# Moving the first mask to ScalarE's DMA queue and redrawing the orders of four engines in a gated cross-attention kernel

## The reference, cut to what matters

```
x        [4, 256, 256]     ctx [4, 1601, 256]     mask [4, 1601] (bytes, one row per batch)
w_gating [2, 256, 1024]    w_linear [1024, 256]   g_xattn, g_ffn: one number each

h      = layernorm(x)
scores = h @ ctx^T / 16, and -1e30 where mask is 0
out    = softmax(scores) @ ctx            (zero if a batch has no key at all)
x      = x + tanh(g_xattn) * out
h2     = layernorm(x)                     (then rounded to fp8 e4m3, as are weights and activations)
x      = x + tanh(g_ffn) * ((gelu(h2 @ w_gating[0]) * (h2 @ w_gating[1])) @ w_linear)
```

## Time and profile before

| | |
|---|---|
| median of 3 runs | 132.19 us (131.89 to 133.86) |
| the profiled execution's own time | 132.56 us |
| its span, first to last instruction | 130.7 us |
| busy: PE / PEld / DVE / ACT / POOL | 123.8 / 106.9 / 102.5 / 77.2 / 87.8 us |
| chain that ended last | PE 81%, DVE 8%, ACT 3%, DMA 3% of the span |
| granted TensorE clock | 1.0 in all 40 slices |
| read from HBM | 11.57 MB |

### The profile page before, as it was taken

The page is one execution under the profiler, slowest core; times in us unless marked ns, Lnnn a source line. Parts: engine busy times, 40 slices in busy tenths (PEclk is TensorE's granted clock), DMA queues, the critical chain, the costliest instruction groups (busy, mean ns, idle before and its releaser), DMA issues.

```text
span 130.7 us, 2554 instructions
## 1 busy us (share of the span) xinstructions
PE 123.8 (95%) x887; PEld 106.9 (82%) x887; DVE 102.5 (78%) x242; ACT 77.2 (59%) x142; POOL 87.8 (67%) x136
## 2 busy tenths in 40 slices
PE   6866999999999999999999999999999999999991
PEld 4545899899999996899999899999989894345780
DVE  3643899687999799995799498999786998966662
ACT  3266478688586799563465896943884306755300
POOL 3077989769939999789999605999949705920000
PEclk9999999999999999999999999999999999999999
DMA  3989998800400316900005000001400000000233
GB/s 103 274 225 367 393 358 347 258 19 3 160 5 0 100 63 212 353 5 0 0 5 160 0 0 0 8 0 7 154 0 5 0 0 0 0 5 10 70 121 120
DMA packets 6915, 12.77 MB, mean 98 GB/s; under 512 B 884, under 2 KB 4728, under 8 KB 6904
## 3 DMA queue, kind: packets, MB, share of 16 engines
q1 hardware_dynamic: 6904, 12.62, 29.0%
HBM read 11.57 MB, written 1.05 MB: 97 GB/s over the span
## 4 chain that ended last, share of the span: by engine, by line
PE 81%; DVE 8%; ACT 3%; DMA 3%; issue 1%; SPq 1%; ACTq 0%; DVEq 0%
PE ring L646 15%; PE pv L678 9%; PE pv L686 9%; PE pv L682 9%; PE scores L660 9%; PE scores L663 8%; PE scores L664 8%; PE scores L707 7%; PE ring L723 5%; DMA cn<-in_ctx_dram 3%; DVE cT_lo L509 2%; ACT cT_hi L422 1%; DVE negm L496 1%; DVE xn L548 1%; ACT gate L449 1%
## 5 line engine op out<-in xcount | busy, mean ns | idle before, releaser
L379 POOL TENSOR_TENSOR chl<-cn,chl 128x256 fp32r<-128x256 f32 (+1 forms) x52 | 37.5, 759 | 7.0 <-ACT chl L429 7.0
L509 DVE TENSOR_TENSOR cT_lo<-ring,cT_hi 128x512 fp32r<-128x512 f32 (+1 forms) x28 | 16.7, 627 | 6.7 <-ACT cT_hi L422 6.7
L663 PE MATMUL scores<-cT_lo,xT_hi 128*128 128x512 f32 (+2 forms) x64 | 21.7, 347 | 0.0
L509 DVE TENSOR_TENSOR pT_lo<-ring,pT_hi 128x512 fp32r<-128x512 f32 (+1 forms) x32 | 18.0, 582 | 4.7 <-ACT pT_hi L422 4.7
L422 ACT ACTIVATE pT_hi<-ring 128x512 fp32r<-128x512 f32 (+1 forms) x32 | 15.5, 511 | 10.5 <-PE ring L646 10.3
L664 PE MATMUL scores<-cT_hi,xT_lo 128*128 128x512 f32 (+2 forms) x64 | 21.7, 345 | 0.0
L422 ACT ACTIVATE cT_hi<-ring 128x512 fp32r<-128x512 f32 (+1 forms) x28 | 14.7, 548 | 9.8 <-PE ring L646 9.8
L660 PE MATMUL scores<-cT_hi,xT_hi 128*128 128x512 f32 (+2 forms) x64 | 18.7, 374 | 1.1 <-ACT cT_hi L422 1.1
L678 PE MATMUL pv<-chl,pT_hi 128*128 128x256 f32 (+1 forms) x104 | 19.2, 297 | 0.0
L387 POOL TENSOR_TENSOR ws<-ws,wc 128x256 f32<-128x256 f32 x24 | 16.2, 707 | 3.8 <-DVE wc L558 3.8
L435 ACT ACTIVATE sp<-sp,nb,sr 128x1024 f32<-128x1024 f32 (+1 forms) x16 | 16.8, 1053 | 1.3 <-DVE nb L525 1.3
(11 more groups left out here) (68 smaller groups left out, 198.4 us busy)
## 6 DMA issues: line engine op xcount, KB each, us to landing
cn<-in_ctx_dram SPq DMA_DIRECT2D x11, 512.0 KB, 7.8
ws<-in_L_ffn_w_gating_dram SPq DMA_DIRECT2D x4, 512.0 KB, 6.8
ws<-in_L_ffn_w_linear_dram SPq DMA_DIRECT2D x2, 512.0 KB, 3.9
out_dram<-xs SPq DMA_DIRECT2D x8, 128.0 KB, 1.7
mrow<-in_mask_BxS_bk_dram SPq DMA_DIRECT2D x4, 200.1 KB, 6.5
xs<-in_x_dram SPq DMA_DIRECT2D x1, 768.0 KB, 9.7
cn<-in_ctx_dram SPq DMA_DIRECT2D x2, 256.0 KB, 3.4
cn<-in_ctx_dram SPq DMA_DIRECT2D x4, 65.0 KB
```

The lines of the kernel that those rows point to most:

```text
L379: last = nc.gpsimd.tensor_tensor(chl[b % 2][0:parts, t, D:2 * D], cn[b % 2][0:parts, t, :], chl[b % 2][0:parts, t, 0:D].bitcast(f32), ALU. ...
L509: nc.vector.tensor_tensor(dst, bank_view(f, size), hi.bitcast(f32), ALU.subtract).then_inc(lo_ready, 1)
L663: nc.tensor.matmul(dst, xT_hi[:, j % (2 * QT), k, :], cT_lo[:, k, cols], start=False, stop=False)
```

## The change

The first mask is no longer loaded by SP between ctx groups 1 and 2. ACT issues it as its first instruction, ahead of everything else on its queue. The second mask moves on SP from behind batch 1's context to behind the first weight piece. All four orders are drawn anew. Cut to its core (each order changes throughout; two lines stand for them):

```diff
     PE_ORDER = """
-        X0:0 X0:1 C0:1 C0:0 S0:0 C0:2 C0:3 C0:4 S1:0 C0:5 S0:1 C0:6 S1:1 X1 S0:2 S0:3 C1:1 C1:0 S1:2 S1:3
+        X0:0 C0:0 X0:1 C0:1 C0:3 C0:2 S1:0 C0:5 C0:6 S1:1 S0:0 C0:4 S0:1 C1:3 C1:0 X1 S0:2 S0:3 S1:2 C1:1
...
     POOL_ORDER = """
-        Z0:0 B0 Z0:1 Z0:3 F1 F0 Z0:2 B1 I0 Z1:1 Z1:3 I1 Z1:2 Z1:0 Z2:3 B2 F2 F3 Z2:1 B3 Q0 I2 Z2:0 Z2:2 Q1
-        Z3:0 I3 Z3:1 Z3:2 Z3:3 Q2 I4 Q3 I5"""
+        F0 B0 Z0:1 Z0:2 Z0:3 Z0:0 F1 B1 I0 Z1:3 I1 Z1:0 Z1:2 Z1:1 F2 B2 Z2:1 Z2:3 Z2:0 Q0 F3 B3 I2 Z2:2 Q1
+        I3 Z3:0 Z3:1 Z3:2 Z3:3 Q2 I4 Q3 I5"""
...
             load_ctx(0, 0)
             load_ctx(0, 1)
-            load_mask(0)
             load_ctx(0, 2)
             load_ctx(0, 3)
             sp_eng.dma_start(xs[:, QT:J, :], x_v[:, QT:J, :]).then_inc(x_in, 16)
             for g in range(NG):
                 load_ctx(1, g)
-            load_mask(1)
...
             load_w(0)
+            load_mask(1)
             load_w(1)
...
+            actor.dma_start(mrow[:, 0, :], mask_BxS2_bk0[0:1, :].broadcast_to([P, K])).then_inc(m_in[0], 16)
             gated = False
             for s in act_order:
```

More of the change, by code:

```diff
@@ L60, in gated_cross_attention_ffn @@
-        S6:3 V4:1 P5:2 P5:1 S7:0 V4:2 S7:2 V4:3 S7:1 P6:1 P6:0 V5:0 S7:3 N1 P6:3 V5:1 V5:2 V5:3 P6:2 P7:3 H0
-        V6:0 P7:1 V6:1 P7:0 V6:2 V6:3 H1 P7:2 V7:0 V7:1 V7:2 V7:3 H2 H3 N2 H4 H5 H6 N3 H7 H8 H9 H10 H11 H12
-        Y0 H13 H14 Y1 H15 Y2 Y3 Y4 Y5 Y6 Y7"""
-    ACT_ORDER = """
[L66 to L71, removed]
@@ L74, in gated_cross_attention_ffn @@
-    DVE_ORDER = """
[L75 to L80, removed]
+        X0:0 C0:0 X0:1 C0:1 C0:3 C0:2 S1:0 C0:5 C0:6 S1:1 S0:0 C0:4 S0:1 C1:3 C1:0 X1 S0:2 S0:3 S1:2 C1:1
@@ new lines, in gated_cross_attention_ffn @@
+        C1:2 S1:3 C1:5 S2:0 P0:0 S2:1 C1:4 P0:1 S3:0 V0:0 C1:6 P0:2 S3:1 P0:3 P1:1 V0:1 P1:0 C2:2 S2:2 C2:1
+        S2:3 P1:2 V0:2 P1:3 C2:0 S3:2 V0:3 S3:3 X2 C2:6 V1:0 C2:5 C2:4 C2:3 V1:1 P2:2 V1:2 V1:3 P2:3 S5:0
+        P2:1 P3:0 S4:0 P2:0 P3:1 X3 S4:1 S5:1 C3:1 V2:0 P3:3 V2:1 S5:2 C3:3 V2:2 V2:3 P3:2 S5:3 S4:2 C3:0
+        S4:3 V3:0 C3:2 C3:6 C3:4 V3:1 V3:2 C3:5 P4:3 V3:3 S6:0 P4:0 N0 P4:1 S6:1 S6:2 P4:2 S6:3 V4:0 P5:3
+        V4:1 S7:0 P5:0 V4:2 N1 V4:3 P6:1 S7:2 P5:2 P6:0 S7:1 P5:1 P6:2 V5:0 S7:3 V5:1 V5:2 V5:3 H0 P7:0 P7:1
@@ new lines, in gated_cross_attention_ffn @@
+        V6:0 P7:2 V6:1 P6:3 V6:2 P7:3 V6:3 H1 H2 V7:0 V7:1 V7:2 V7:3 H3 H4 H5 N2 H6 N3 H7 H8 H9 H10 H11 H12
+        H13 Y0 Y1 H14 H15 Y2 Y3 Y4 Y5 Y6 Y7"""
+    ACT_ORDER = """
+        X0:0 C0:0 X0:1 C0:1 R0:1 C0:3 C0:2 R0:3 C0:6 C0:5 R0:2 K1 C0:4 R0:0 C1:3 C1:0 X1 R1:2 C1:1 C1:2 E0:0
+        C1:5 E1:1 E1:0 P0:0 C1:4 E0:1 P0:1 C1:6 P0:2 R1:1 P0:3 P1:1 R1:3 K2 P1:0 C2:2 C2:1 P1:2 R1:0 P1:3
+        C2:0 E2:1 X2 C2:6 C2:5 E2:0 C2:4 C2:3 P2:2 E3:0 K3 R2:3 P2:3 P2:1 P3:0 R2:1 P2:0 R2:2 P3:1 X3 E3:1
+        R2:0 C3:1 P3:3 C3:3 P3:2 C3:0 E5:1 C3:2 E4:1 C3:6 E4:0 C3:4 C3:5 P4:3 P4:0 N0 R3:1 P4:1 R3:3 R3:2
+        P4:2 P5:3 E5:0 E6:1 E6:0 P5:0 N1 P6:1 R3:0 P5:2 P5:1 P6:0 P6:2 E7:0 E7:1 H0 P7:0 P7:1 P6:3 P7:2 P7:3
+        H1 H2 H3 H4 N2 H5 H6 N3 H7 H8 H9 H10 H11 H12 H13 H14 H15"""
@@ new lines, in gated_cross_attention_ffn @@
+    DVE_ORDER = """
+        G0:0 G0:1 X0:0 C0:0 X0:1 C0:1 C0:3 C0:2 C0:6 G1 C0:5 M1:0 C0:4 M0:0 C1:3 C1:0 X1 M0:1 C1:1 C1:2 M1:1
+        C1:5 W0 W1 P0:0 C1:4 G2 P0:1 C1:6 P0:2 M2:0 P0:3 P1:1 M3:0 P1:0 C2:2 C2:1 M2:1 P1:2 A0 P1:3 C2:0 X2
+        C2:6 M3:1 C2:5 G3 C2:4 U0 C2:3 P2:2 A1 P2:3 P2:1 P3:0 U1 W2 P2:0 P3:1 M5:0 X3 P3:3 C3:1 M4:0 A2 M5:1
+        P3:2 C3:3 C3:0 M4:1 U2 C3:2 C3:6 L0 C3:4 C3:5 P4:3 A3 U3 P4:0 M6:0 P4:1 M6:1 P4:2 L1 W3 P5:3 P5:0 A4
+        P6:1 P5:2 P5:1 M7:0 M7:1 W4 P6:0 A5 P6:2 U4 H0 P7:0 P7:1 U5 P6:3 A6 W5 L2 P7:3 P7:2 H1 U6 H2 A7 U7
+        H3 H4 L3 H5 H6 H7 H8 H9 H10 H11 Y0 H12 Y1 H13 H14 Y2 H15 Y3 Y4 Y5 Y6 Y7"""
```

## The result

| | before | after |
|---|---|---|
| median | 132.12 us (131.89 to 133.86) | 133.65 us (132.79 to 134.09, four executions) |
| profiled execution, its span | 132.56, 130.7 us | 133.42, 131.6 us |

The ratio is 1.013, with an interval of 1.010 to 1.016: slower by 1.3%, where 0.5% was forecast. The experiments came in three groups (runs 1 to 4, 5 to 8 and 9 to 12), each with its own executions of before (medians 131.55, 131.99 and 132.13); compare within a group. Executions that took over 1.5% longer than the fastest of the same kernel (one of 136.17 us of the control among them) are left out of the ratios.

The account below looks back on a forecast made before the run. PE, busy 123.8 of 130.7 us, was taken as the bound, its continuous run opened by group 2's landing. 132.56 + 0.2 + 0 + 0.4 = 133.2, or 132.8 on the median's footing; 8 in 10 range 131.2 to 134.5.

Parts of the forecast that it names:

- the forecast case: Whole kernel: the summed terms hold, 132.8 us on the median's footing, from 132.1 to 133.6; chance 0.5.
- its own signs: Profile after: prediction wrong if group 2 lands a microsecond off or a batch change shows an unnamed PE wait.
- On ACT it is free: Start: the mask's 0.43 us issue, moved from SP to ACT, costs nothing, ACT being idle 2.88 us before its first copy.
- I take 0.6, since nothing else in that early stretch is as slow: Start: the mask in front pushes back x and group 0 by 0.6 us, or 1.7 at the old slump's rate; covered.
- I keep its landing at 11.9: Start: context group 2 lands at 11.9 us as before, the bytes ahead of it being the same.
- Rival 1: Start: the slump goes with the mask, landings, PE's run and G1 come 1.3 us earlier, 131.5 us; chance 0.22.
- Start: +0.2: Start: PE's run begins at 12.1 as before, then X1 waits 0.2 us for DVE near 18.5.
- Middle: 0: Batch changes: the old hole at G3 goes (-0.3), a new wait of 0.3 us opens at P0:3 near 32.
- I see it covered: Middle: the old 0.3 us hole behind G3 vanishes, two weighted sums now standing beside G3.
- End: +0.4: End: N3 at T + 4.7 (T: V7's end), H4's bank free only after A7; PE waits 1.0, regains 0.6.
- Rival 2: DVE comes late to fills: G2's place costs 1.3 not 0.3, the end's 0.6 isn't regained, 134.4 us; chance 0.18.
- Rival 3: Start: the mask in front holds up x and group 0, at most 1.7 us against 1.9 cover; 133.3; chance 0.05.

Follow-up runs that it names:

- the control: The changed kernel itself, measured again unaltered: 134.00 us, ratio 1.018 to the kernel before.
- run 4: The changed kernel without any load of the first mask, VectorE setting its bytes to 1: 134.05 us, ratio 1.018 to the kernel before.
- runs 10 and 11: The changed kernel with an unread 200 KB load in the first mask's place: 128 different rows (135.94 us), then one row 128 times (133.72 us).
- run 6: The changed kernel with 22 instead of 15 warm-up matmuls on zeros: 132.89 us, ratio 1.012 to the kernel before.
- Run 9: The changed kernel with 22 warm-up matmuls and, on DVE, W5 moved from behind A6 to behind L3: 132.20 us, ratio 1.000 to the kernel before.
- run 7: The changed kernel with 22 warm-up matmuls, H2 back behind V7 and A7, L3 ahead of H4's product: 133.63 us, ratio 1.016 to the kernel before.
- run 12: The kernel before with the first mask loaded behind context group 2 and 22 instead of 15 warm-up matmuls: 131.78 us, ratio 0.996 to the kernel before.

## Why the prediction was right or wrong

The sign was right, and 133.65 lies in the range; the forecast case itself (132.1 to 133.6) was just missed. By its own signs, though, the prediction was wrong: group 2 landed 2.0 us off, and a batch change (V6) shows a PE wait that I hadn't named. That the sum still came near is luck in part, as the steps show:

- **"On ACT it is free"**: right. ACT idles 4.12 us before its first copy.
- **"I take 0.6, since nothing else in that early stretch is as slow"**: the mis-sized term of the start. x came 1.8 us later, about my upper bound of 1.7. A repeated row is slow in front as well (runs 4, 10 and 11), so the price in the old stretch, 1.7, was the one to take. The argument that the second mask went at 327 GB/s misled; why that one was fast no run shows (more transfers were perhaps in flight).
- **"I keep its landing at 11.9"**: wrong by 2.0 us. 0.5 of it is SP's issue of the mask, which I had taken off SP and then not off group 2. The other 1.5 is that the bytes ahead of group 2 were the same but their time wasn't. Rival 1 (the slump goes with the mask) named this, and its own objection, that a slow mask in front only moves the slump, is what happened at the front: group 2, G1 and bias came earlier, x later. But run 4 has a slump at 6 to 7 us without any mask, and gets only 0.8 of the 1.5; the other 0.7 no run explains. Of the 2.0 us, 0.6 reached the run of PE, because PE came to the fill at 11.48; with the longer warm-up it comes there at 10.75 (run 6).
- **"Start: +0.2", the wait at X1**: not there; start -0.6. G1 came 1.5 earlier and DVE was ahead.
- **"Middle: 0"**: the wait at P0:3 didn't come, and **"I see it covered"**, of the hole at G3, failed: 0.36 us remained, behind one DVE instruction of 1.81. With 0.17 at V6 (96.75), where A5 stands behind W4, and 0.33 of busy time, the middle is +0.5. Start and middle together are -0.1, where +0.2 was forecast: right in sum, by two errors that cancel.
- **"End: +0.4"**: mis-sized, +1.0. The form was right: N3 waits 0.83 (1.0 forecast), nothing behind it, 0.59 regained (0.6). But N3 starts at T + 5.3, not T + 4.7. The step that failed is "free only after A7" "by the same durations": W5, now beside POOL's additions, took 1.75 us instead of 1.11, H2's product stood ahead of A7 too, and A7 slid from T + 0.3 to T + 0.96. Run 9 shows it; run 7 shows that H2's place alone doesn't mend it.
- **Rival 2** (DVE late to the fills): its place at P0:3 was wrong, its kind right at the end. **Rival 3**: the mask in front did hold up x, by 1.8 us, just within the cover of 1.9; the first scores (10.01) were no later than the 10.3 that I had walked. The cover held against the landing, not against the clock. By the rule it cites (the Trainium skill, page DMA: Bandwidth & Descriptors, section Queues, rings and completion order) any 200 KB in front would delay x alike; runs 10 and 11 put 0.8 us on that and 1.8 on the repetition.
- **What I left out altogether** is the clock. A late x leaves 1.4 to 2.0 us of idle PE behind the warm-up, and PE comes to full rate only at 9.25 us (10.12 in the control) instead of 5.45. That cost 0.7 us in the profile after and 1.1 in the control (against runs 9 and 7 at equal landings), hidden in my account by group 2's earlier landing.

Open: why one row read 128 times is slow (the runs show that, not the mechanism); where the last 0.7 us of group 2's earlier landing come from; the 0.33 us of busy time; and why the 0.69 of run 12's start brings only 0.35 of time.

## What to carry to other kernels

Cost a transfer by what it did to its neighbours, not by its bytes: a load that repeats a row can slow what is in flight beside it, so try it behind the loads that the engines wait for, and look whether the slump goes with it. Whoever makes the first input later should lengthen PE's warm-up to reach it, and read the durations of the first matmuls, not the clock column alone. And when steps are moved on an engine that shares time with another, look again at everything queued ahead of the one instruction that PE waits for: a filler moved there costs its contended duration, not the one in the old trace.
